# Edge columns and the isolated sources' rows moved to earlier stages of a four-layer graph kernel

## The chip, the cores and the metric

One core of a Trainium2 chip runs the whole program in one launch. The metric is device time in microseconds. The kernel before was run three times; its median is 2548.24 us.

## The reference

Four graph layers follow each other on 50,000 nodes of 128 features with 25,000 edges, sorted by destination. Each layer's result is added to its input and normalized by row (`_layernorm`).

```python
x = _layernorm(x + gat_two_layers(x, src, dst, ...))        # layer 1: two attention layers, 4 heads of 16, then 1 of 128
x = _layernorm(x + mean_of_sources(x @ W.T, src, dst) + b)   # layer 2: mean over incoming edges
m = relu(concat(x[dst], edge_attr) @ W1 + b1) @ W2 + b2      # layer 3: one message per edge
x = _layernorm(x + mean(m) @ Wm + bm + max(m) @ Wx + bx + sum(m) @ Ws + bs)
x = _layernorm(x + gat(x, src, dst, W, att, bias))           # layer 4: attention
```

A node that is no edge's destination gets only the biases in every layer. Its row can be made from its own input row alone; a source of this sort is called isolated here.

## The kernel before, in words

Edges are handled in NG = 49 groups of 512 (GT = 4 tiles of 128), not in 98 blocks of nodes. Sums over the edges of one destination are running scans along the sorted edges (`tensor_tensor_scan` on VectorE), so rows are turned into columns by transposes on PE, scanned, multiplied and turned back. The stages are separated by barriers over all five engines. Each engine's program is written out in its own order, and engines meet only in semaphores.

- **prep** (0 to 32 us) and **a** (32 to 541): indices, weights, gathers of x by source and destination.
- **b** (590 to 757, after a softmax): first attention layer in columns. `pipeline` runs `rates_vector`'s first step and `map_table` between two groups of the loop.
- **c** (757 to 1045): for each group, `look` on PE and `pick` on VectorE find the position of each source in the edge list, `hid` writes the indices, and GpSimd gathers those rows (`c_pool`, four gathers a group). Beside it VectorE and ScalarE make rows of x1 for isolated sources (`shifted`, `apply`), and VectorE runs in between what `extra` lists: the bias rows, two more edge rates and four node rates. VectorE's turn g is `hot(g+1)`, `pick(g)`, `shifted(g)`, `hid(g)`. `hot(g+1)` waits for the source digits `slb` of group g+1, which SP loads (L1457). SP's turn g is: load digits g, load rows g, store rows g-2 (L1465).
- **d** (1068 to 1285, after a softmax): second attention layer. Beside it, `local_tensor`, `local_scalar` and `local_sync` make the isolated sources' rows for layer 4: a transpose of the factors, two wide products (L1506, L1507), four scaled copies (L1524), a load and a store.
- **e** (1285 to 1564): layer 2. GpSimd gathers four times a group (L658), PE turns the rows and multiplies (L1647, L1655), VectorE scans, adds, normalizes; SP stores x2 as rows.
- **f** (1564 to 1985): layer 3, over the groups in reverse. SP loads rows of x2 and the edge features, PE turns both (`turn`), VectorE spreads each destination's last row over its edges (`spread`), PE makes hidden units and messages, VectorE scans totals and maxima (`totals`), PE combines in columns (`combine`), ScalarE and VectorE take the two results out (`columns`, L1817 and L1878), PE turns them back (`rows`, L1779), and `residual` and the normalization finish; GpSimd scatters.
- **g** and **h** (to 2540): layer 4. The change doesn't touch them.

`pipeline(engine, stages)` runs each stage in the given order for group g minus its lag, so (2, rows) works on the group two turns back. `count(engine, name, i, j, lag)` waits for the semaphore of the group `lag` back.

## Time and profile before

| | |
|---|---|
| median of 3 runs | 2548.24 us (2527.15 to 2566.37) |
| the profiled execution | 2542.37 us, span 2540.6 us |
| mean granted clock of TensorE | 0.679 |
| busy share of the span | PE 75%, VectorE (DVE) 68%, GpSimd (POOL) 54%, ScalarE (ACT) 43% |
| mean DMA rate | 157 GB/s |

Busy shares are averages over stages with different limits. A clock of 1.00 is 2.4 GHz, 0.50 is 1.2 GHz. In the timelines below each row has the start, the duration, the engine and line, what it wrote and read, and in brackets how long the engine had been idle and what ended that.

### The profile page before, as it was taken

What the parts mean: (1) busy time and instruction counts of PE and PEld (TensorE: products, weight loads), DVE (VectorE), ACT (ScalarE), POOL (GpSimd) and SP (SyncE); (2) the same over time, 40 slices, a digit from 0 to 9 for tenths busy, and PEclk for the clock granted to TensorE, in tenths of its full rate; (3) what the DMA queues carried; (4) which work ended last, traced back from release to release, by engine and by line L of the source; (5) the groups of instructions that cost most, each with busy time, mean ns of one, the idle gap of its engine ahead of it and who ended that gap; (6) DMA issues with size and microseconds to landing.
All of it is one profiled execution on the core that took longest, in us unless ns stands there. A gap on an engine that the chain in (4) does not pass through costs nothing.

```text
span 2540.6 us, 30997 instructions
## 1 busy us (share of the span) xinstructions
PE 1895.0 (75%) x7398; PEld 1202.8 (47%) x7398; DVE 1740.2 (68%) x6542; ACT 1083.8 (43%) x3008; POOL 1383.0 (54%) x1388
## 2 busy tenths in 40 slices
PE   3999999867874445399944454999998699959983
PEld 2898888855651112155534342444444122225542
DVE  6444445458769966598768885888887366678773
ACT  0222222215753343287633332666665455524332
POOL 4777777720006577200057771566666677727776
PEclk9656656655556665599756856999999555556565
DMA  4555555553334455288645554333332699933341
GB/s 154 160 155 157 155 152 160 159 188 133 125 127 125 112 156 160 72 278 262 211 131 155 154 159 120 98 112 111 109 106 82 237 363 326 313 105 100 122 135 37
DMA packets 255479, 398.63 MB, mean 157 GB/s; under 512 B 80999, under 2 KB 97536, under 8 KB 255172
## 3 DMA queue, kind: packets, MB, share of 16 engines
q1 hardware_dynamic: 204340, 307.86, 37.2%
q0 software_dynamic: 43904, 75.95, 11.0%
q10 hardware_dynamic: 7056, 12.85, 1.4%
q8 instruction: 62, 1.02, 0.2%
q14 instruction: 117, 0.96, 0.1%
HBM read 225.25 MB, written 178.97 MB: 159 GB/s over the span
## 4 chain that ended last, share of the span: by engine, by line
POOL 17%; issue 12%; PE 9%; DVE 9%; ACT 7%; DMA 3%; SPq 1%; POOLq 0%; DVEq 0%; ACTq 0%
POOL ring L658 9%; POOL big L658 4%; POOL out_dram L664 4%; ACT outr L720 3%; DVE big L1870 2%; ACT big L1809 2%; PE bank L1570 2%; DVE stats L674 2%; PE bank L1507 2%; PE bank L1506 2%; DMA ring<-x_t,idx 1%; PE bank L1211 1%; DVE z L1886 1%; DMA hT<-xsrc_e 1%; DVE mv L683 1%
## 5 line engine op out<-in xcount | busy, mean ns | idle before, releaser
L720 ACT ACTIVATE outr<-z,rn 128x128 f32<-128x128 f32 x784 | 322.7, 483 | 347.9 <-DVE rn L709 155.7
L658 POOL DMA_INDIRECT ring<-in_x_dram,idx x392 | 380.0, 969 | 147.3 <-issue 119.3
L658 POOL DMA_INDIRECT ring<-x_t,idx x280 | 269.0, 961 | 339.6 <-SPq L302 245.3
L658 POOL DMA_INDIRECT ring<-hidden_e,idx x196 | 193.3, 986 | 298.9 <-DVE idx L1361 241.6
L664 POOL DMA_INDIRECT x_t<-outr,idx x196 | 234.6, 1197 | 208.4 <-ACT outr L720 162.0
L1148 DVE TENSOR_TENSOR_SCAN G<-cont,G,bank 64x512 f32<-64x512 uint8 (+1 forms) x192 | 242.8, 1265 | 80.0 <-PE bank L1211 57.2
L664 POOL DMA_INDIRECT out_dram<-outr,idx x196 | 195.2, 996 | 102.7 <-issue 58.2
L1947 PE MATMUL bank<-DB,z 20*128 20x512 f32 x196 | 201.7, 1131 | 22.8 <-DVE xT L1337 7.0
L1020 DVE BATCH_NORM_STATS2 stats<-ring 128x6 f32<-128x128 f32 x196 | 42.8, 281 | 247.9 <-DMA ring<-in_x_dram,idx 247.9
L1301 PE MATMUL bank<-table,hT 128*128 128x391 bf16 x196 | 94.3, 481 | 153.4 <-DVE hT L1345 153.4
L674 DVE BATCH_NORM_STATS2 stats<-z 128x6 f32<-128x128 f32 x784 | 171.0, 281 | 5.1
L1211 PE MATMUL bank<-ident,msg 128*64 128x128 f32 (+1 forms) x588 | 136.3, 377 | 35.1 <-DVE msg L1133 32.2
L1570 PEld LDWEIGHTS bank<-W_s,G 65*128 65x128 f32 (+1 forms) x784 | 130.4, 252 | 65.4 <-issue 64.1
L1647 PE MATMUL bank<-ident,ring 128*128 128x128 f32 x196 | 47.8, 389 | 138.6 <-DMA ring<-x_t,idx 138.6
L1570 PE MATMUL bank<-W_s,G 65*128 65x128 f32 (+1 forms) x784 | 147.6, 348 | 0.0
L938 PEld LDWEIGHTS bank<-bT,msg 128*128 128x128 f32 x784 | 146.1, 277 | 1.0 <-ACT msg L977 0.9
L938 PE MATMUL bank<-bT,msg 128*128 128x4 f32 x784 | 143.5, 306 | 0.7 <-ACT msg L977 0.7
L977 ACT ACTIVATE msg<-bank 128x512 f32<-128x512 f32 x98 | 58.6, 598 | 188.8 <-PE bank L928 188.8
L1917 DVE CUSTOM_DVE_ANT_0 msg<-ring,attb 128x128 f32<-128x128 f32 x280 | 63.9, 288 | 101.9 <-DMA ring<-x_t,idx 59.3
L1211 PEld LDWEIGHTS bank<-ident,msg 128*64 128x64 f32 (+1 forms) x588 | 82.1, 163 | 93.1 <-issue 43.9
L658 POOL DMA_INDIRECT big<-x_t,idx x112 | 107.1, 956 | 34.2 <-issue 34.2
L716 ACT ACTIVATE sd<-mv,epsc 128x4 f32<-128x4 f32 x196 | 56.3, 287 | 157.8 <-DVE mv L683 157.8
(385 smaller groups left out, 4516.7 us busy)
## 6 DMA issues: line engine op xcount, KB each, us to landing
hT<-in_x_dram SPq DMA_DIRECT2D x194, 256.0 KB
ring<-x_e SPq DMA_DIRECT2D x147, 256.0 KB, 2.9
x_t<-outr SPq DMA_DIRECT2D x98, 256.0 KB, 2.7
x_e<-outr SPq DMA_DIRECT2D x98, 256.0 KB, 2.1
x_t<-xload SPq DMA_DIRECT2D x48, 512.0 KB, 3.1
xsrc_e<-ring SPq DMA_DIRECT2D x49, 256.0 KB, 2.1
xd_e<-ring ACTq DMA_DIRECT2D x49, 256.0 KB, 2.9
ring<-xsrc_e SPq DMA_DIRECT2D x49, 256.0 KB
```

The source lines that it names most:

```text
L658: nc.gpsimd.indirect_dma_start(to(c), None, table, bass.IndirectOffsetOnAxis(ap=idx[:, kind, (g + 1) * GT + c:(g + 1) * GT + c + 1].bitcas ...
L664: nc.gpsimd.indirect_dma_start(table, bass.IndirectOffsetOnAxis(ap=idx[:, kind, (g + 1) * GT + c:(g + 1) * GT + c + 1].bitcast(U32), axis= ...
L674: ins = v.bn_stats(stats[:, k, :], z[:, s, k, :])
L720: ins = nc.scalar.activation(to[:, k, :], frm[:, k, :], ACT.Identity, bias=sc[:, k, 1:2], scale=sc[:, k, 0:1])
L938: ins = nc.tensor.matmul(bank[4 + g % 2][:, at:at + 4], dxT[:, h, k * P:(k + 1) * P], bT[:], start=True, stop=True)
L977: nc.scalar.activation(dxT[:, q % 2, :], bank[0][:], ACT.Copy).then_inc(S("n_dxT"), 1)
L1148: return v.tensor_tensor_scan(o, m, src_ap, ini, ALU.mult, ALU.add)
L1211: ins = nc.tensor.transpose(bank[s][0:width, c * P:(c + 1) * P], msg[:, s, c, 0:width], ident[:])
L1301: nc.tensor.matmul(o, lhs, table[:, 0, :], start=True, stop=False)
L1570: ins = nc.tensor.matmul(bank[2 + s][:, c * F:(c + 1) * F], G[0:k, s, c * P:(c + 1) * P], W[:], start=not b, stop=not b or c == GT - 1)
L1917: c.do(v.tensor_tensor_reduce(msg[:, n, k, :], frm, attb[:, n, :], 1.0, 0.0, ALU.mult, ALU.add, dots[:, k, n:n + 1]))
L1947: nc.tensor.matmul(bank[2 + q % 4][:], ecT[q % 4], DB[0:GT * CN, :, :].rearrange("p t f -> p (t f)"), start=True, stop=True).then_inc(S("o ...
```

## The change

Two pieces of work move to an earlier stage, and layer 3 is rearranged around what then lies in memory.

1. The isolated sources' layer-4 rows go from d to c. They use the rows that c loads anyway (`rload`), so a load goes; a transpose, two wide products, a copy and four scaled copies go to PE and ScalarE of c, and a second store to SP of c. The edge rates and bias rows which they need go from c to b. `look` has five banks in place of six.
2. Stage e no longer stores x2 as rows. PE turns the normalized rows (`back`) and the edge features (`edges`) into columns, ScalarE copies them, and SP stores both as columns.
3. Stage f loads columns; its `turn` and the edge copy go. `combine` now has the group's columns as the stationary operand, so that it gives rows, with the two sums side by side in one bank; x2 plus bias is added by a product with the identity. The transposes back and both `columns` copies go, one copy with bias on ScalarE (`f_xb`) comes. The order of the stages on each engine is changed.

```diff
+            edge = rates_vector(v, 3, "e", ecov, est, alpha3, est, etemps)
             pipeline(v, [(-1, weighing(v, "b", feat, HF, HEADS)), (2, join), (0, scanning(v, "b", HF))],
-                     [rates_vector(v, 3, "e", ecov, est, alpha3, est, etemps)[0], map_table(v)])
+                     [edge[0], map_table(v), edge[1], rows_of_biases(v), edge[2]])
...
+        def local_tensor(pe):
+            def factors(g):
+                need(pe, "s_ecT", g)
+                nc.tensor.transpose(bank[6][0:GT * CN, 0:P], ecov[:, four(g), :].rearrange("p t k -> p (t k)"),
+                                    ident[:]).then_inc(S("s_tr"), 1)
+
+            def local(g):
+                s = g % 2
+                wait(pe, f"c_ld{g % RING}", 16 * (g // RING + 1))
+                need(pe, "s_ecT", g + 1)
+                need(pe, "s_row", g - 1)
+                nc.tensor.matmul(bank[5 + 2 * s][:], ident[:], rload[:, g % RING].rearrange("p t f -> p (t f)"), start=True, stop=False)
+                nc.tensor.matmul(bank[5 + 2 * s][:], hcT[g % 4], DB[0:GT * CN, :, :].rearrange("p t f -> p (t f)"),
+                                 start=False, stop=True).then_inc(S("s_mm"), 1)
+            return factors, local
+
+        def local_scalar(a):
...
+            def local(g):
+                need(a, "s_mm", g + 1)
+                if g >= 2:
+                    wait(a, f"s_out{g % 2}", 16 * (g // 2))
+                for k in range(GT):
+                    ins = nc.scalar.activation(sx[:, g % 2, k * F:(k + 1) * F], bank[5 + 2 * (g % 2)][:, k * F:(k + 1) * F],
+                                               ACT.Copy, scale=alpha3[:, GT * g + k:GT * g + k + 1])
+                ins.then_inc(S("s_row"), 1)
+
+        def local_store(sp, g):
+            need(sp, "s_row", g + 1)
+            sp.dma_start(edge_row(x3s_e, g), sx[:, g % 2, :]).then_inc(S(f"s_out{g % 2}"), 16)
...
             for g in range(NG):
                 look(g)
...
+                factors(g)
+                if g:
+                    local(g - 1)
+            local(NG - 1)
...
             for g in range(NG + 1):
                 if g in extra:
                     extra[g]()
                 if g < NG:
+                    factors(g)
+                if g:
+                    local(g - 1)
+                if g < NG:
                     apply(g)
...
             for g in range(NG + 2):
                 if g < NG:
                     load(g)
...
                 if g >= 2:
                     store(g - 2)
+                    local_store(sp, g - 2)
...
-            pipeline(pe, [(0, turn), (1, project)])
+            def edges(i, j):
...
+                for c in range(GT):
+                    ins = nc.tensor.transpose(bank[6 + s][0:EF, c * P:(c + 1) * P], e_ea[:, s, c, :], ident[:])
...
+            def back(i, j):
...
+                for c in range(GT):
+                    ins = nc.tensor.transpose(bank[4 + s][:, c * P:(c + 1) * P], outr[:, j, c, :], ident[:])
+                ins.then_inc(S("e_xtr"), 1)
+            pipeline(pe, [(0, turn), (1, project), (1, edges), (3, back)])
...
+            return (0, load), (4, store)
...
+                nc.scalar.activation(e_eaT[:, s, :], bank[6 + s][0:EF, :], ACT.Copy).then_inc(S("e_eaT"), 1)
...
+                nc.scalar.activation(e_xT[:, s, :], bank[4 + s][:], ACT.Copy).then_inc(S("e_xT"), 1)
+            pipeline(a, [(2, step), (2, edges), (4, back)])
...
+                sp.dma_start(f_x[:, j], x2T_e[g]).then_inc(S(f"f_xs{j}"), 16)
+                count(sp, "f_m1", i, j, RING)
+                sp.dma_start(f_ea[:, j], eaT_e[g]).then_inc(S(f"f_xs{j}"), 16)
...
-                nc.tensor.matmul(bank[4][:], Mm_s[:], G[:, s, :], start=True, stop=True)
-                nc.tensor.matmul(bank[5][:], Ms_s[:], G[:, s, :], start=True, stop=False)
-                nc.tensor.matmul(bank[5][:], Mx_s[:], MX[:, s, :], start=False, stop=True).then_inc(S("f_mm2"), 1)
...
+                for c in range(GT):
+                    o = f_rows(s, c)
+                    e = slice(c * P, (c + 1) * P)
+                    nc.tensor.matmul(o[:, 0:2 * F], G[:, s, e], MmMs[:], start=True, stop=False)
+                    nc.tensor.matmul(o[:, F:2 * F], MX[:, s, e], Mx_s[:], start=False, stop=False)
+                    ins = nc.tensor.matmul(o[:, F:2 * F], aT[:, s, e], ident[:], start=False, stop=True)
+                ins.then_inc(S("f_mm2"), 1)
+            pipeline(pe, [(-1, hidden), (0, message), (1, combine)])
+
+        def f_rows(s, c):
+            return bank[4 + s + 2 * (c // 2)][:, (c % 2) * 2 * F:(c % 2 + 1) * 2 * F]
...
-                nc.scalar.activation(aT[:, s, :], bank[4][:], ACT.Copy).then_inc(S("f_aT"), 1)
+                nc.scalar.activation(aT[:, s, :], X2T[:, j, :], ACT.Identity, bias=m3c[:]).then_inc(S("f_xb"), 1)
...
-            pipeline(a, [(0, relu), (-1, edges), (3, apply), (0, message), (2, means), (1, columns), (2, root)])
+            pipeline(a, [(-1, relu), (0, message), (3, apply), (0, columns), (2, means), (2, root)])
...
-                v.scalar_tensor_tensor(bT2[:, s, :], bank[5][:], m3c[:], X2T[:, j, :], ALU.add, ALU.add) \
-                    .then_inc(S("f_bT"), 1)
...
-            pipeline(v, [(3, scale), (-1, spread), (0, penalty), (0, totals), (2, residual), (2, norm_stats(v, "f")),
-                         (2, norm_var(v, "f")), (1, columns)])
+                for n in range(2):
+                    rows = bank[4 + s + 2 * n][:].rearrange("p (t n f) -> p t n f", t=2, n=2)[:, :, 1, :]
+                    ins = v.tensor_tensor(z[:, s, 2 * n:2 * n + 2], rows, zA[:, s, 2 * n:2 * n + 2], ALU.add)
+                ins.then_inc(S("f_z"), 1)
+            pipeline(v, [(3, scale), (-2, spread), (0, penalty), (0, totals), (2, residual), (2, norm_stats(v, "f")),
+                         (2, norm_var(v, "f"))])
```

## Rows read from the trace of the kernel before

**Rows 1.** Windows: us; busy PE, PEld, DVE, ACT, POOL (count); clock, DMA, GB/s.

```profile
757.00:1045.00 288.00, 121.53 (x392) 46.78 (x392) 212.40 (x658) 106.09 (x301) 193.28 (x196) 0.62 0.49 135
...
1068.00:1284.50 216.50, 206.52 (x833) 110.90 (x833) 176.27 (x637) 148.39 (x491) 0.00 (x0) 0.85 0.75 237
1284.50:1564.00 279.50, 120.70 (x588) 107.20 (x588) 218.41 (x839) 90.11 (x245) 188.70 (x196) 0.65 0.51 151
1564.00:1985.00 421.00, 370.66 (x1372) 186.93 (x1372) 330.24 (x784) 250.40 (x637) 234.58 (x196) 0.96 0.33 98
...
1100.00:1130.00 30.00, 29.80 (x138) 16.13 (x138) 28.81 (x105) 24.13 (x82) 0.00 (x0) 1.00 0.89 283
```

**Rows 2.** Instructions of one line, f: duration ns, first and last start us.

```profile
L1148 DVE TENSOR_TENSOR_SCAN G<-cont,G,hT x48: 1282/1284/1337, 1582.1 to 1952.6; 128x512 f32<-128x512 uint8 x48
```

**Rows 3.** Timeline of stage f, one group and the next scan.

```profile
1743.33 0.38 DVE L683 BATCH_NORM_AGGREGATE mv<-stats 128x2 f32<-128x6 f32 x4
...
1743.62 0.72 DVE L1878 SCALAR_TENSOR_TENSOR big<-bank,m3c,big 128x512 f32<-128x512 f32 x1
1743.74 0.30 ACT L716 ACTIVATE sd<-mv,epsc 128x4 f32<-128x4 f32 x1 [2.06 <-DVE mv L683]
...
1744.99 1.64 ACT L720 ACTIVATE outr<-z,rn 128x128 f32<-128x128 f32 x4
...
1745.35 1.02 PE L1759 MATMUL bank<-hT,M_s 128*128 128x512 f32 x2
...
1746.53 0.67 ACT L1800 ACTIVATE hT<-bank,m2c 128x512 f32<-128x512 f32 x1
...
1747.10 1.12 ACT L1809 ACTIVATE big<-bank,invR 128x128 f32<-128x128 f32 x4
1747.24 1.28 DVE L1148 TENSOR_TENSOR_SCAN G<-cont,G,hT 128x512 f32<-128x512 uint8 x1 [1.07 <-ACT hT L1800]
```

**Rows 4.** Timeline of stage c: GpSimd around the node layers, then one ring.

```profile
810.87 0.94 POOL L658 DMA_INDIRECT ring<-hidden_e,idx  x1 [0.57 <-DVE idx L1361]
...
870.70 2.66 POOL L658 DMA_INDIRECT ring<-hidden_e,idx  x1 [2.85 <-DVE idx L1361]
...
908.25 0.95 POOL L658 DMA_INDIRECT ring<-hidden_e,idx  x1 [0.30 <-issue]
...
916.47 0.42 ACT L1427 ACTIVATE big<-ring 128x256 f32<-128x256 f32 x1 [4.85 <-DMA ring<-hidden_e,idx]
...
918.55 0.32 SPq L1465 DMA_DIRECT2D x_t<-outr  x1
...
919.50 0.42 ACT L1427 ACTIVATE big<-ring 128x256 f32<-128x256 f32 x1 [0.97 <-DMA ring<-hidden_e,idx]
...
923.19 0.35 DVE L1345 TENSOR_SCALAR hT<-hT,pcol 128x512 bf16<-128x512 bf16 x1 [3.54 <-DMA hT<-srclo_d]
...
926.49 0.16 DVE L1361 SCALAR_TENSOR_TENSOR idx<-hidt,dhi 128x4 int32<-128x4 f32 x1
```

**Rows 5.** Timeline of stage d: its last scan.

```profile
1270.53 1.27 DVE L1148 TENSOR_TENSOR_SCAN G<-cont,G,bank 64x512 f32<-64x512 uint8 x1 [2.69 <-PE bank L1211]
```

**Rows 6.** Groups by line: busy us, mean ns, idle before.

```profile
L1240 ACT ACTIVATE hT<-G,b1c 64x512 f32<-64x512 f32 x49 | 34.6, 706 | 0.0
...
L1886 DVE TENSOR_TENSOR z<-bank,big 128x512 f32<-128x512 f32 x49 | 32.7, 667 | 5.6 <-ACT big L1809 5.6
...
L1129 DVE TENSOR_TENSOR msg<-big,alpha 128x256 f32<-128x256 f32 x49 | 19.2, 394 | 0.1
...
L1379 DVE SCALAR_TENSOR_TENSOR DB<-biasc,ident,DB 32x128 f32<-32x128 f32 x12 | 4.1, 340 | 0.4
```

**Rows 7.** Timeline of stage b: PE behind a rate layer.

```profile
667.83 1.97 PE L1221 MATMUL bank<-W2x,hT 64*128 64x66 f32 x8 [8.09 <-DVE hT L1199]
```

**Rows 8.** Timeline of stage e: residual and mask.

```profile
1412.34 1.13 DVE L1671 SCALAR_TENSOR_TENSOR z<-bank,invR,ring 128x128 f32<-128x128 f32 x4 [0.36 <-PE bank L1655]
...
1414.11 0.16 DVE L709 TENSOR_TENSOR rn<-rn,lastR 128x8 f32<-128x8 f32 x1
```

More of the change, by code:

```diff
@@ L1191, in map_table, with rows_of_biases, step @@
             return step
+        def rows_of_biases(v):
+            ch = Chain(v)
+            def step():
+                for t in range(GT):
+                    for k, n in ((0, 1), (1, 2), (2, 3), (3, None), (4, 0)):
+                        row = ones[0:32, :] if n is None else biasc[0:32, n, :]
+                        at = ident[0:32, CN * t + k:CN * t + k + 1]
+                        if k == 0:
+                            ch.link(v.tensor_scalar(DB[:, t, :], row, at, None, ALU.mult))
+                        else:
+                            ch.link(v.scalar_tensor_tensor(DB[:, t, :], row, at, DB[:, t, :], ALU.mult, ALU.add))
+            return step
         def b_vector(v):
@@ L1369, in shifted @@
                     .then_inc(S("c_z"), 1)
-            def rows_of_biases():
-                for t in range(GT):
-                    for k, n in ((0, 1), (1, 2), (2, 3), (3, None), (4, 0)):
-                        row = ones[0:32, :] if n is None else biasc[0:32, n, :]
-                        at = ident[0:32, CN * t + k:CN * t + k + 1]
-                        if k == 0:
-                            ch.link(v.tensor_scalar(DB[:, t, :], row, at, None, ALU.mult))
-                        else:
-                            ch.link(v.scalar_tensor_tensor(DB[:, t, :], row, at, DB[:, t, :], ALU.mult, ALU.add))
-            edge = rates_vector(v, 3, "e", ecov, est, alpha3, est, etemps)
             node = rates_vector(v, 4, "n", cross, stat, alpha4, None, ntemps)
@@ L1387, in scaled @@
                 v.sem_inc(S("n_scaled"), 1)
-            extra = {3: rows_of_biases, 5: edge[1], 7: edge[2], 9: node[0], 11: node[1], 13: node[2], 15: node[3],
-                     16: scaled}
+            extra = {9: node[0], 11: node[1], 13: node[2], 15: node[3], 16: scaled}
             hot(0)
@@ L1573, in attend_tensor @@
             wait(pe, tag + "_ones", 1)
[L1574 to L1578 removed]
+            pipeline(pe, [(0, turning(pe, tag, width)), (1, project)])
         def attend_scalar(a, tag, stored):
@@ L1586, in step @@
                 norm_apply(z[:, s], outr[:, j], rn[:, s]).then_inc(S(tag + "_row"), 1)
-            if tag == "d":
-                factors, local = local_scalar(a)
-                pipeline(a, [(-1, factors), (1, local), (0, step)])
-            else:
-                groups(a, step)
+            groups(a, step)
         def attend_pool(pool, tag, table, kind, rev):
@@ L1624, in linear_sync @@
             if more is None:
-                pipeline(sp, [(-2, load), (3, store)] + list(also))
+                pipeline(sp, [(-2, load)] + ([(3, store)] if to is not None else []) + list(also))
             else:
@@ L1689, in step, with edges, back @@
                 count(a, "e_st", i, j)
-                slot_done(a, "e_out", i, j, 16, 1)
+                need(a, "e_xtr", RING * i + j + 1 - RING)
                 norm_apply(z[:, s], outr[:, j], rn[:, s]).then_inc(S("e_row"), 1)
-            groups(a, step)
-        eaR = ring[:, 0:2, 1, :, 0:EF]
+            def edges(i, j):
+                g = RING * i + j
+                s = g % 2
+                need(a, "e_eatr", g + 1)
+                if g >= 2:
+                    wait(a, f"e_out{(g - 2) % RING}", 16 * ((g - 2) // RING + 1))
+                nc.scalar.activation(e_eaT[:, s, :], bank[6 + s][0:EF, :], ACT.Copy).then_inc(S("e_eaT"), 1)
+            def back(i, j):
+                g = RING * i + j
+                s = g % 2
+                need(a, "e_xtr", g + 1)
+                if g >= 2:
+                    wait(a, f"e_xo{(g - 2) % RING}", 16 * ((g - 2) // RING + 1))
+                nc.scalar.activation(e_xT[:, s, :], bank[4 + s][:], ACT.Copy).then_inc(S("e_xT"), 1)
+            pipeline(a, [(2, step), (2, edges), (4, back)])
+        f_x = ring[:, :, 0].rearrange("p s t f -> p s (t f)")
+        f_ea = ring[0:EF, :, 1].rearrange("p s t f -> p s (t f)")
         def f_sync(sp):
@@ L1727, in store @@
                 sp.dma_start(edge_row(x3_e, g), outf[:, j, :]).then_inc(S(f"f_out{j}"), 16)
-            pipeline(sp, [(-1, load), (3, store)])
+            pipeline(sp, [(-3, load), (3, store)])
             for j in range(RING):
@@ L1732, in f_tensor @@
         def f_tensor(pe):
[L1733 to L1745 removed]
             def hidden(i, j):
[L1748 removed]
                 count(pe, "f_spread", i, j)
[L1750 removed]
+                wait(pe, f"f_xs{j}", 32 * (i + 1))
                 count(pe, "f_relu", i, j, 1)
                 nc.tensor.matmul(bank[2][:], M1a[:], X2T[:, j, :], start=True, stop=False)
[L1753 removed]
+                nc.tensor.matmul(bank[2][:], M1b[:], f_ea[:, j], start=False, stop=True).then_inc(S("f_m1"), 1)
             def message(i, j):
@@ L2014, in _ @@
             barrier(sp)
-            linear_sync(sp, "d", xd_e, x1_e, False, "_z", also=local_sync(sp))
-            for s in range(2):
-                sp.wait_ge(S(f"s_out{s}"), 16 * len(range(s, NG, 2)))
+            linear_sync(sp, "d", xd_e, x1_e, False, "_z")
             barrier(sp)
-            linear_sync(sp, "e", x1_e, x2_e, False, "_z")
+            linear_sync(sp, "e", x1_e, None, False, "_z", also=e_turn_sync(sp))
+            for j in range(RING):
+                wait(sp, f"e_out{j}", 16 * (BODIES + (j == 0)))
+                wait(sp, f"e_xo{j}", 16 * (BODIES + (j == 0)))
             barrier(sp)
```

237 lines of the change are left out of this document (65 added, 172 removed), and 2 rows, old and new, of the table SHARED.

## Prediction

> **What bounds the kernel now.** I read the windows by stage first, then in each stage the change touches the timeline of a few groups, asking which wait ends last. The span is 2540.6 us; the profiled execution as a whole took 2542.4 us, 5.9 under the median of 2548.2 shown. The change touches stages b to f [rows 1]. In **f** VectorE starts its totals scan every 7.88 us ((1952.6 - 1582.1) / 47) [rows 2]. VectorE is not full: it waits 1.07 us for ScalarE's message in each group [rows 3]. The reader is to see a ring: VectorE adds m3c (L1878), PE transposes the rows and only then makes the message (L1759), ScalarE adds its bias (L1800), VectorE scans, and so back to L1878 [rows 3]. In **c** each gather takes 0.95 us and the next follows after 0.30, so four make 5.0 us a group. GpSimd is just about the bound, but a second ring has little slack. For one group it reads: gather issued from 908.25, rows copied at 916.47, mean layer's apply, SP's store at 918.55, then SP's load of the source digits, for which VectorE waits until 923.19, index ready at 926.65 [rows 4]. That is 18.4 us for four groups' time, 20.0: the copy of group g-4 releases the index of group g, because apply(g-2) stands behind copy(g-4) on ScalarE and the digits of g+1 stand behind store(g-2) on SP. In **d** the windows show PE busy 207 of 216 us, and VectorE 28.8 of 30 us where the clock is 1.00 [rows 1]. In **e** GpSimd issues the gathers at 1.25 us, 5.0 us a group, and VectorE is busy 218 of 280 us [rows 1, 4].
>
> **Stage f.** VectorE loses `columns` (0.72 us, 0.64 from its start to the next) and gets the residual in two halves. A 128x512 one takes 0.67, a 128x256 operation 0.39, so two cost 0.79, 0.12 more [rows 6]. But `columns` was what covered the square root between the variances and the next reciprocal: from the start of the variances (1743.33) to the end of the root (1744.04) is 0.71, where `columns` started after 0.29 [rows 3]. So 7.89 - 1.07 - 0.64 + 0.12 + 0.45 = 6.75, with what the halves add in starts 6.8. ScalarE's order changes too: apply and a copy from SBUF now stand between message and means. From the variances' start: root at 0.41, relu 0.2 later, message and apply 0.57 after each (1747.10 - 1746.53), so apply 1.75, columns 3.29 (1.54 for apply, from 1744.99 to 1746.53), then 0.63 (the nearest row, a 64x512 from SBUF, takes 0.71 with its tail) and four means of 1.12 together: ready at 5.05, just where VectorE wants them (5.02: 0.74 to the reciprocal, 0.31 for the scale, 1.6 for spread and penalty, 2.37 for the two totals scans) [rows 3, 6]. PE: column passes fall from 8192 to 7168 a group, so its busy 7.56 (370.7 / 49) becomes at most 6.6, and the clock, 0.96, stays as the load does [rows 1]. I take 6.83: (7.88 - 6.83) x 47 = 49 saved; bounds 6.65 and 7.15, which are 58 and 34. The transposes that vanish from the start are made good by one more stage of lead. The loads sit behind the same 3.1 MB of `cont`.
>
> **Stage d.** It loses a transpose, two wide products and five ScalarE instructions a group. From its first scan, 1.4 us into the stage, to its last at 1270.53 there are 48 steps of 4.19 us [rows 1, 5]. At full clock 105 VectorE instructions in 30 us are 8.1 groups of 13, 3.71 each [rows 1]. VectorE's work does not depend on the clock, and what PE keeps (four transposes, four fp32 products in two passes each, twelve passes of 128 columns) fits 3.7 us even at half the clock: a pass of 512 takes 0.43 at the upper level (1.02 for two with their tail [rows 3]), so one of 128 at the lower 0.21, and twelve 2.6. 48 x 0.48 = 23 saved, and about 6 in the drain, where two wide products at half clock went before the last rows: 29; bounds 22 and 33.
>
> **Stage b.** It gains two rate layers and the twenty instructions for the bias rows. The rate layer that is there held up the product by 8.09 us [rows 7]; the two others are shorter (one and no later term): 7 and 6. Twenty instructions of 0.34 plus a wait each are 7.4, less 0.7 of VectorE's slack in a group [rows 6]. The index table, moved to the middle, no longer waits for its prefix products at the end, about 3.5. Sum 7 + 6 + 6.7 - 3.5 = 16 lost; bounds 12 and 20.
>
> **Stage c.** What it loses on VectorE is worth about 4 us, since GpSimd ran on. What it gains is: on PE a transpose and two wide fp32 products; on ScalarE a copy of the factors and four scaled copies (together some 1.3 us); on SP one more 256 KB store a group. None is long. The costly part is **where they stand**. `local_store(g-2)` waits for ScalarE's `local(g-2)`, which is in ScalarE's turn g-1, behind copy(g-3). Behind that wait on SP are the digits of g+1, and behind those VectorE's index of g. So the ring that spanned four groups spans three. Its length: from gather to copy 8.2; copy, factors and local 1.7, where apply had 2.1; stores 0.4 and digits 4.3; hot, pick, shift and index 3.5: 18.1 us [rows 4], or 6.05 a group in place of 5.0. When the gather lands quickly (group 25 began at 913.25 and was copied at 919.50, 6.3 against 8.2) it is 16.2, or 5.4. I take 6.05, because the burst of SP's transfers now follows every copy and meets the gather in flight. Eight groups (9 to 17) take 59.8 us, 810.87 to 870.70 [rows 4], bound by VectorE's node layers, and don't change. Three start without the ring. The 48 steps from the first group's gather to the last's are 270 of the stage's 288 us (9 go by before the first index, 9 from the last gather on) [rows 1]; they become 59.8 + 15 + 37 x 6.05 = 299: 29 lost. Bounds: 5.4 gives 4, and 7.0 gives 64.
>
> The clock is the other term in c. Now it is 0.62 with PE busy 122 of 288 us; in d, nearly full, 0.85; in f 0.96 [rows 1]. 
> **Stage e.** PE gets eight transposes, ScalarE two copies (0.58 and 0.60), SP a load and a second store. Two things could end the cover. On ScalarE the next root now stands behind apply and both copies: 1.54 + 0.5 + 0.5 + 0.33 = 2.9 us from the start of apply to the reciprocal, 0.1 to the residual, 1.77 from there to the mask (1412.34 to 1414.11) and 0.2 to the next apply: 4.9 in all against 5.0, so I cost them at nothing [rows 3, 8]. PE's work at half clock is twenty passes of 128, 4.3 us of 5.0. The drain gets a transpose, a copy and a store: 3 lost; bounds 0 and 18. The transfers add 256 KB a group to a DMA share of 0.51 [rows 1]. The edge rows are 256 bytes each; the Trainium skill ("DMA: Bandwidth & Descriptors", Specifications) gives 512 B as the least transfer for line rate. By that rule this load costs about twice its bytes, still within the free share, so it speaks for the fourth rival alone; no row of e shows it, since such loads run only in f.
>
> **Sum.** 16 + 29 - 29 + 3 - 49 = -30. Against the profiled execution 2512; against the median of the runs 2518. All bounds at once give -75 and +46; they won't all fall together.
>
> **Rivals.** (1) The ring in c doesn't bind and GpSimd sets 5.0 a group. For it: SP's waits cost others little now, and in every second group the gather lands fast. Against it: the count of turns above. 59.8 + 40 x 5.0 is 10 less than before: -69, so 2479. (2) The other side: the burst (256 KB store, digits, 256 KB load) lengthens its own ring. The digits and the gather then land some 2 us later each, 21.9 in place of 18.1, 7.3 a group: c loses 75 and the sum is +16, 2564. It decides from 6.86 a group on, where c has eaten the rest. Against it: the DMA share in c is 0.49. (3) In f the means come late (ScalarE's longer order, a dearer SBUF copy): 7.3 a group, 22 us less gain, 2540. (4) The edges aren't hidden beside e's gathers: ScalarE's chain of 4.9 or the small rows make 5.5 a group, 24 us more, 2542; then the change doesn't do what it says.
>
> **Chances.** Forecast 0.45 with its own range of 2495 to 2540; rivals 0.20, 0.12, 0.13 and 0.10. A measurement of this kernel can tell about 2% (51 us) from no change. Faster by more is most of rival 1 and the forecast's low edge, 0.26; slower by more needs rival 2 and a second mishap, 0.06. The range goes from rival 1 to past rival 2, with the 20 us by which the runs differ.
>
> **What the changed profile would show.** f: totals scans 6.8 us apart, no wait of VectorE for ScalarE's message, 0.4 us of wait before the reciprocal. c: outside the node layers 6.05 between groups, GpSimd waiting for the index in each, VectorE waiting for the digits, SP waiting for the sx copies. d: scans 3.7 apart at whatever clock. e: still 1.25 between gathers. I am wrong if c stays at 5.0 (rival 1), if PE's clock in f falls below 0.9, or if e's gathers show gaps.

## The result and the profile after

The changed kernel is slower, by 1.2 to 2.2%. In four runs of each, side by side, its median is 2570.4 us (2569.7 to 2574.1) and that of the kernel before 2537.7 (2520.9 to 2566.4); the ratio is 1.017, 95% interval 1.012 to 1.022. Here and below, medians are of all executions, while ratios and their intervals leave out those more than 1.5% above the fastest of the same kernel. The two profiled executions differ by 28 us: 2570.8 against 2542.4 us, spans of 2569.0 and 2540.6.

The table gives each stage in these two profiles. The marks are the first scan of stage b, VectorE's first hot mask (the start of c's lookups), its last one, the first scan of e, the last one, the first running maximum of f, and the first dot product of g.

| stretch | before | after | change | predicted |
|---|---|---|---|---|
| b, first scan to first hot mask | 168.1 | 185.3 | +17 | +16 |
| c, first to last hot mask | 264.6 | 306.9 | +42 | +29 |
| rest of c and d, to e's first scan | 268.7 | 231.9 | -37 | -29 |
| e, first to last scan | 244.1 | 297.0 | +53 | 0 |
| e's drain and f's start | 41.3 | 48.2 | +7 | +3 |
| f, from its first maximum to g | 417.7 | 368.0 | -50 | -49 |

The rest (a before, g and h behind) differs by 4 us in the other direction, and with it the rows add up to the 28 us of the spans. Four terms are about where they were put. Two are not: c, and above all e.

The windows of the changed kernel, to be read against [rows 1]; the rows are stages b, c, d, e and f.

```profile
core 0: us, PE busy (x) PEld busy (x) DVE busy (x) ACT busy (x) POOL busy (x), PEclk, DMA share, GB/s
587.00:772.00 185.00, 143.91 (x589) 114.06 (x587) 131.87 (x205) 116.17 (x254) 0.00 (x0) 0.51 0.28 108
772.00:1092.00 320.00, 242.17 (x637) 82.27 (x637) 200.23 (x625) 164.56 (x541) 188.83 (x196) 0.73 0.55 160
1092.00:1303.00 211.00, 139.61 (x602) 117.98 (x602) 184.78 (x667) 99.33 (x253) 0.83 (x2) 0.50 0.38 124
1303.00:1627.50 324.50, 184.04 (x980) 166.11 (x980) 218.41 (x838) 142.05 (x343) 187.25 (x196) 0.69 0.56 159
1627.50:2024.00 396.50, 344.56 (x1481) 211.95 (x1481) 309.76 (x784) 232.43 (x607) 243.84 (x204) 0.91 0.39 120
```

In e (fourth row) no engine is near full: VectorE does the same 218 us of work as before in 45 us more, and GpSimd's 187 us of gathers are spread over 324. So something else ends last there. The waits of the changed kernel from e's first scan to its last say what (us in total, times, longest):

```profile
PE bank L1615 <- ACT hT L1689: 105.9, 41, 4.6
ACT outr L720 <- DVE rn L709: 99.9, 46, 3.3
DVE rn L692 <- ACT sd L716: 76.9, 41, 3.2
ACT hT L1689 <- DMA eaT_e<-hT: 56.3, 43, 2.6
...
POOL ring L658 <- PE bank L1597: 43.7, 23, 3.0
```

The fourth row is the root and the others are what it drags along. ScalarE's copy of the edge columns (L1689) waits in 43 of 49 groups for the store of the columns two groups back to land. (The landing of a transfer is meant from its issue to the release of the engine that waits for it.) TensorE's next edge transposes wait for that copy, VectorE's reciprocal for the root behind it, and GpSimd's gathers for TensorE's turn (L1597), which is the gap between gathers that the prediction named as the sign of its being wrong.

The timeline of the changed kernel, one turn in e:

```profile
1445.73 0.59 ACT L1689 ACTIVATE hT<-bank 64x512 f32<-64x512 f32 x1 [1.89 <-DMA eaT_e<-hT]
1446.22 0.58 ACT L1697 ACTIVATE hT<-bank 128x512 f32<-128x512 f32 x1
1446.83 0.32 SPq L1648 DMA_DIRECT2D x2T_e<-hT  x1
1447.19 0.43 SPq L1557 DMA_DIRECT2D ring<-x_t  x1
1447.67 0.50 SPq L1637 DMA_DIRECT2D hT<-in_edge_attr_dram  x1
1448.21 0.49 SPq L1646 DMA_DIRECT2D eaT_e<-hT  x1
1449.48 0.94 POOL L658 DMA_INDIRECT ring<-x_t,idx  x1 [2.64 <-PE bank L1597]
1453.33 0.59 ACT L1689 ACTIVATE hT<-bank 64x512 f32<-64x512 f32 x1 [2.59 <-DMA eaT_e<-hT]
```

It is a ring of **one** turn. The copy (1445.73), the back copy behind it on ScalarE (1446.22), SyncE's store of the node columns, which waited for the back copy (1446.83), two loads behind that store, and only then the store of the edge columns (1448.21), whose landing releases ScalarE's next copy (1453.33). From copy to issue is 2.5 us in all but the last few turns; from issue to the next copy it is 5.1 us here, 4.4 and 3.0 in the turns on either side. The 49 copies run from 1325.55 to 1621.57, 6.2 us apart, so the landing takes 3.7 on average. The chain of waits that ended last, over the same stretch, says the same in one line, for the changed kernel and then for the kernel before:

```profile
by line: DMA eaT_e<-hT 51.1%; issue 11.4%; POOL ring L658 8.1%; ACT hT L1697 7.9%; SPq L1637 6.5%; SPq L1557 5.7%; SPq L1648 4.2%; DMA ring<-x_t,idx 1.4%; ACT hT L1689 0.7%; PE bank L1605 0.6%; ACTq L291 0.5%; DVE z L1661 0.4%; PE bank L159
```
```profile
by line: POOL ring L658 74.2%; issue 23.5%; DMA ring<-x_t,idx 1.2%; POOLq L302 0.5%; PE bank L1647 0.5%; PE bank L1655 0.3%
```

Before, GpSimd's gathers and the gaps between them are 98% of the chain. After, the landing and the five instructions of the ring are three quarters. Over the whole stage the landings that a copy waits for take 2.3 to 5.1 us, 3.8 in the mean. The Trainium skill ("DMA: Bandwidth & Descriptors", Anatomy of one DMA) gives, for transfers issued by GpSimd, about 2.0 us of fixed cost, most of it the write's receipt, and the bytes at 436 GB/s: 2.3 us for these 128 KB, an estimate by that page. The trace is above it in every turn shown, and comes down to it only once, at the end of the stage. This store is in flight beside gathers and behind 640 KB that SyncE issued just ahead. The 256 KB store of the node columns, which has no other issue close ahead of it, lands in 2.1 us (median) in the same stage; that what stands ahead makes the difference is likely, and not shown.

In c the predicted ring is there. In the changed kernel, SyncE's store of the isolated rows (L1345) stands ahead of the digits (L1475), and VectorE's mask (L1386) waits for them; compare [rows 4]:

```profile
956.62 1.09 ACT L1338 ACTIVATE xT<-bank,dlo 128x128 f32<-128x128 f32 x4
957.73 0.32 SPq L1345 DMA_DIRECT2D x_t<-xT  x1
958.10 0.43 SPq L1475 DMA_DIRECT2D hT<-srclo_d  x1
958.26 0.16 DVE L1402 SCALAR_TENSOR_TENSOR idx<-hidt,dhi 128x4 int32<-128x4 f32 x1
...
961.98 0.35 DVE L1386 TENSOR_SCALAR hT<-hT,pcol 128x512 bf16<-128x512 bf16 x1 [3.55 <-DMA hT<-srclo_d]
```

### The profile page after: what moved, and what is told of

Read it like the earlier page. It is cut to its first block, busy times and chain, and to the rows that moved or that the text cites. A ratio compares the mean times of both kernels' runs of the same rounds, so it can differ in the third digit from the quotient of the medians.

```text
span 2569.0 us, 32122 instructions
## 1 busy us (share of the span) xinstructions
PE 1978.2 (77%) x7888; PEld 1327.5 (52%) x7888; DVE 1715.9 (67%) x6541; ACT 1125.9 (44%) x3061; POOL 1379.5 (54%) x1388
## 4 chain that ended last, share of the span: by engine, by line
DVE 12%; POOL 11%; issue 10%; ACT 9%; DMA 8%; PE 3%; SPq 2%; POOLq 0%; ACTq 0%; DVEq 0%
DMA eaT_e<-hT 6%; POOL out_dram L664 4%; POOL big L658 4%; DVE stats L674 3%; ACT outr L720 3%; POOL ring L658 3%; DVE G L1148 2%; ACT big L1777 2%; DVE z L1847 1%; DVE mv L683 1%; DVE z L1512 1%; DMA ring<-x_t,idx 1%; ACT big L1785 1%; ACT hT L1697 1%; ACT hT L1763 1%
## 5 line engine op out<-in xcount | busy, mean ns | idle before, releaser
L1226 PE MATMUL bank<-ident,msg 128*64 128x128 f32 (+1 forms) x588 | 154.1, 417 | 68.6 <-DVE msg L1133 65.6
L1528 PEld LDWEIGHTS bank<-W_s,G 65*128 65x128 f32 (+1 forms) x784 | 166.2, 312 | 65.8 <-issue 63.4
L1528 PE MATMUL bank<-W_s,G 65*128 65x128 f32 (+1 forms) x784 | 183.7, 411 | 0.4 <-DVE G L1148 0.4
L1355 PE MATMUL bank<-table,hT 128*128 128x391 bf16 x196 | 87.4, 446 | 72.1 <-DVE hT L1386 71.3
L1226 PEld LDWEIGHTS bank<-ident,msg 128*64 128x64 f32 (+1 forms) x588 | 89.6, 177 | 102.9 <-DVE msg L1133 81.0
L1615 PE MATMUL bank<-ident,hT 128*64 128x128 f32 x196 | 42.2, 357 | 110.0 <-ACT hT L1689 110.0
L1749 PE MATMUL bank<-MmMs,G 128*128 128x256 f32 x392 | 121.4, 392 | 6.7 <-DVE z L1847 3.3
```

Of the source, the lines that this page charges most:

```text
L1226: ins = nc.tensor.transpose(bank[s][0:width, c * P:(c + 1) * P], msg[:, s, c, 0:width], ident[:])
L1355: nc.tensor.matmul(o, lhs, table[:, 0, :], start=True, stop=False)
L1528: ins = nc.tensor.matmul(bank[2 + s][:, c * F:(c + 1) * F], G[0:k, s, c * P:(c + 1) * P], W[:], start=not b, stop=not b or c == GT - 1)
L1749: nc.tensor.matmul(o[:, 0:2 * F], G[:, s, e], MmMs[:], start=True, stop=False)
```

## Experiments

All are compared with the kernel before, run beside them. The first nine kernels met a condition that the first pair had not: every kernel, the one before too, took 2.91 to 2.97 ms, with idle time on VectorE, ScalarE and TensorE at once that nothing in the trace releases (see the last section). In the eight after that the kernel before was back at 2536 and 2543 us. Both are told, since the first kernels misled me about c. "Distance" is the mean time between VectorE's scans (e) or hot masks (c).

### First set: one limit at a time

**The store of the edge columns one turn earlier.** SyncE issues it as soon as the copy is done, ahead of that turn's wait for the back copy:

```
+            def store_ea(i, j):
...
+                need(sp, "e_eaT", g + 1)
+                sp.dma_start(eaT_e[g], e_eaT[:, g % 2, :]).then_inc(S(f"e_out{j}"), 16)
...
-            return (0, load), (4, store)
+            return (0, load), (3, store_ea), (4, store)
```

> In the changed kernel ScalarE's copy of a group's edge columns waits 44 times for the landing of the store of the columns two groups back (56.5 us in all). SyncE issues that store behind the store of the node columns of the turn before, which itself waits for ScalarE, so the wait closes a ring of one turn. Here the store of the edge columns is issued one turn earlier and nothing else changes. Theory (the ring sets stage e): the forward scans come 5.0 to 5.3 us apart instead of 6.19, ScalarE's waits for that landing fall below 10 us, and the time falls by 42 to 57 us, to 2513 to 2528 us. Rival (the waits fill time that transfers at a share of .56 and a TensorE clock of .69 cost anyway): the scans stay above 5.9 us and the time at 2555 us or more.

Measured: distance 6.38 us in e, no wait for that landing among the large ones, 2923.4 us, ratio 0.991 (0.986 to 0.995).

**The same store first in its turn.** It stays at lag 4 but goes ahead of the two loads.

> A smaller dose of the same. The store of the edge columns stays at its turn but goes ahead of that turn's two loads (0.43 + 0.50 us of issue). The ring of one turn stays and loses about 1.0 us. Theory: scans 5.1 to 5.4 us apart, time lower by 38 to 52 us than the changed kernel, and some wait for the landing stays (10 to 40 us in all). Rival (transfers and clock): scans above 5.9 us, time at 2555 us or more. A second rival (SyncE's order matters by what is queued ahead in the queues, not by the time of issue) would give the same as the run with the earlier turn, with no wait left.

Measured: 6.50 us, 2940.9 us, ratio 0.993 (0.988 to 0.998). The distances of both runs are on the side of the rival (above 5.9 us). The times say nothing by themselves, since both theory and rival had been worked out for the conditions of the first pair.

**c: the store of the isolated rows one turn later.**

```
-            for g in range(NG + 2):
+            for g in range(NG + 3):
...
-                if g >= 2:
+                if 2 <= g < NG + 2:
                     store(g - 2)
-                    local_store(sp, g - 2)
+                if g >= 3:
+                    local_store(sp, g - 3)
```

> Only stage c changes: the store of the isolated sources' rows goes three turns behind the loads instead of two, so that it no longer holds the next digits load until ScalarE's rows of the turn before are done. Theory (a ring of three groups, 20 us long, sets c): the ring has four groups again, hot masks come 5.2 to 5.9 us apart instead of 6.65, first to last gather 274 to 295 us instead of 314, time lower by 19 to 40 us than the changed kernel (2530 to 2551 us). Rival (TensorE at 1.2 GHz, with 8.6 us of matmuls a group at that clock, sets c): first to last gather stays at 300 us or more and the time at 2556 us or more.

Measured: 6.55 us in c, 2949.0 us, ratio 0.998 (0.995 to 1.001). The expectation gives 6.65 us for the changed kernel; its masks of the first profile are 6.39 us apart, so this is no gain at all.

**Both edits.**

> Both edits together. Theory: they are in different stages and add up, 61 to 97 us less than the changed kernel, 2473 to 2509 us, that is 1 to 3% faster than the kernel before. Rival (one or both of the rings were not what set their stages): 2520 us or more.

Measured: 6.60 us in c, 6.51 in e, 2941.4 us, ratio 0.993 (0.989 to 0.997). Taken alone, this set spoke for the rivals. What was missing were the unaltered kernels under the same conditions.

### Second set: the unaltered kernels, and what is left in e

> The changed kernel once more, unaltered, so that the next three have it beside them on the same chip and day. Scans of stage e 6.2 to 6.7 us apart, hot masks of stage c 6.3 to 6.7, ratio to the kernel before 1.00 to 1.02 whatever the theory.

Measured: 6.64 us in e, 6.39 in c, 2933.7 us, ratio **0.994** (0.990 to 0.998). Under these conditions the change doesn't lose, against the expectation's 1.00 to 1.02.

> With the edge columns' store one turn earlier the scans of stage e were still 6.38 us apart, against 6.63 in a run with that stage unaltered, and the waits had moved: TensorE's edge transposes now wait 20 times for the landing of the attributes' load, which SyncE issues one turn ahead behind the node columns' store. Here that load goes two groups ahead as well, into four buffers instead of two (the store of the edge columns stays one turn earlier). Theory (ScalarE's back copy, SyncE, a landing, TensorE or ScalarE again: rings of one or two turns through SyncE's order set the stage): scans 5.0 to 5.5 us apart, time 33 to 55 us under the changed kernel on this chip. Rival (the gathers of this stage with a transfer share of .56, and TensorE's clock, set it): still 6.1 us or more, time less than 20 us under it.

```
-                need(sp, "e_eatr", g - 1)
+                need(sp, "e_eatr", g - 3)
...
-            return (0, load), (4, store)
+            return (-2, load), (3, store_ea), (4, store)
```

Measured: 6.33 us, 2923.8 us, ratio 0.992 (0.988 to 0.995): 10 us under the changed kernel, which is the rival's figure.

> Leaves out of stage e all work on edge attributes (their load, the four transposes, ScalarE's copy and the store); stage f then loads raw attributes in place of their columns, so its messages are of other numbers at the same sizes. What is left in stage e of the move are the node columns. Theory (the edge columns' ring is what stage e lost): scans 5.0 to 5.4 us apart, time 38 to 60 us under the changed kernel. Rival (the node columns' part, four transposes, a copy of 0.58 us and a 256 KB store, costs as much or more): 5.8 us or more, time less than 25 us under it.

Measured: 6.13 us, 2915.2 us, ratio 0.987 (0.981 to 0.993): 19 us under it, the rival's figure too.

> Stage c with the rows' store at three turns and without the matmul of the identity with the loaded rows (1.9 us a group at 1.2 GHz, 1.0 at 2.4), so that the isolated sources' rows lack the sources' own part. With the store at three turns alone the hot masks came 6.55 us apart, no closer than before. Theory (the ring of three groups and TensorE at 1.2 GHz lie level at 6.5 to 6.7 us a group, so that one edit alone shows nothing): 5.2 to 5.9 us apart, time 25 to 55 us under the changed kernel. Rival (landings of the digits and of the gathers set the stage, whatever TensorE does): 6.3 us or more, time less than 12 us under it.

Measured: 6.33 us in c, 2934.3 us, ratio 0.994 (0.990 to 0.998): no change, again the rival's figure.

> The kernel before once more, unaltered, for its profile. In the runs so far both kernels take 2.93 to 2.97 ms where the first pair took 2.54 and 2.57, and the changed kernel's profile of those runs has idle time ahead of an engine that ends with nothing that the trace shows, up to 22 us long, which its first profile has not. Theory (instructions arrive late there, in both kernels): this profile has such gaps too, stage a some 200 us longer than in the first profile of this kernel, and the scans of stage e 5.6 to 6.4 us apart in place of 4.98, since a stage that was set by its engines' own work loses more by it than one that waits for landings anyway. Rival (the gaps belong to the changed kernel's code): no such gaps, scans 5.0 us apart.

Measured: 2963.4 us; the same kernel beside it took 2912.8, so one execution here can be 50 us off another. e 6.01 us (5.09 in the first profile, where the expectation, dividing 47 steps by 48, has 4.98), c 6.08, stage a 211 us longer than in the first profile, b within 1 us and f's maxima 7.81 us apart as they were. Waits of ScalarE over the whole run, kernel before, in the first profile and then in this one:

```profile
ACT msg L977 <- PE bank L928: 188.8, 98, 9.9
```
```profile
ACT msg L977 <- remote: 175.4, 21, 14.4
ACT z L1960 <- issue: 132.5, 77, 13.6
ACT outr L720 <- issue: 129.8, 62, 4.0
```

So all of e's changes must be read between 6.01 (before) and 6.64 (after): 6.64 unaltered, 6.50 store first, 6.38 store a turn earlier, 6.33 load earlier too, 6.13 without edges, 6.01 before. Each is one profile. The store a turn earlier came out again in the kernel with both edits, at 6.51, so differences of 0.13 us say nothing, while three profiles with an unaltered e agree within 0.03 (6.63 to 6.66). The edges are 0.51 of the 0.63 us, and the ring 0.13 to 0.26 of them. It binds, but other idle time covers most of it.

### Third set: doubling the suspected cost

```
+                sp.dma_start(eaT2_e[g], e_eaT[:, s, :]).then_inc(S(f"e_out{j}"), 16)
                 sp.dma_start(eaT_e[g], e_eaT[:, s, :]).then_inc(S(f"e_out{j}"), 16)
```

> The changed kernel with the store of the edge columns issued twice, the second to a tensor that nobody reads, and ScalarE's copy waiting for both. It lengthens the ring of one turn by one issue of 0.5 us and by what the landing of 128 KB more takes. Theory (the ring binds in most groups): the scans of stage e come 0.5 to 1.2 us further apart than in the unaltered changed kernel of these runs (6.64), so 7.1 to 7.8 us, time 20 to 55 us longer than it. Rival (transfer load alone): under 6.9 us, the same growth as in the next run.

> The same doubling in the kernel in which that store goes one turn earlier (6.38 us between scans). Theory: the landing has a turn to spare there, so the doubling costs only what the extra transfer takes from others, 0 to 0.3 us a group. Rival (transfer load sets the stage): the scans move apart by as much as in the run before.

These ran without that idle time. Doubled in place: 2594.6 us, ratio 1.026 (1.019 to 1.034). Doubled with the store a turn earlier: **2516.1 us, ratio 0.994** (0.990 to 0.998), 54 us under the changed kernel although it stores 128 KB more in every group. (The changed kernel's 2570.4 us are of the first pair, whose kernel before took 2537.7; here it took 2536.1.) The scans of e in the kernel before, in the changed kernel, then in these two (first and last start after the commas):

```profile
L1148 DVE TENSOR_TENSOR_SCAN G<-cont,G,bank x48: 1246/1280/1282, 1298.5 to 1537.7; 128x512 f32<-128x512 uint8 x48
```
```profile
L1148 DVE TENSOR_TENSOR_SCAN G<-cont,G,bank x48: 1246/1248/1282, 1315.4 to 1608.2; 128x512 f32<-128x512 uint8 x48
```
```profile
L1149 DVE TENSOR_TENSOR_SCAN G<-cont,G,bank x48: 1245/1248/1281, 1318.1 to 1630.2; 128x512 f32<-128x512 uint8 x48
```
```profile
L1149 DVE TENSOR_TENSOR_SCAN G<-cont,G,bank x48: 1244/1249/1281, 1319.0 to 1559.8; 128x512 f32<-128x512 uint8 x48
```

Counted from the first scan of all, which these lines leave out, the distances are 5.09, 6.19, 6.59 and 5.10 us. In the ring the second store costs 0.40 us a group, less than the 0.5 to 1.2 expected: about its issue of 0.5 us, and no time of its own to land. Outside the ring it costs nothing. The rival's "under 6.9 us" is met, its "same growth" in the second kernel is not, and that is what tells the two apart: transfer load as the cause is out. ScalarE's wait for the landing, in the kernel doubled in place, against 56.3 us above:

```profile
ACT hT L1691 <- DMA eaT_e<-hT: 77.1, 43, 2.9
```

> Part 1 of the change alone (the isolated sources' rows beside stage c) on the kernel before. By the stages of the two unaltered kernels in runs of this kind: stage b 16 us longer, stage c's hot masks 15 us longer in all, from the last of them to the first scan of stage e 52 us shorter, so 18 to 24 us less than the kernel before. If the parts act on each other (for instance through TensorE's clock), the stages come out otherwise. In the first pair the same stages add up to 23 us more.

Measured: 2562.4 us, ratio 1.014 (1.006 to 1.021), so slower, not faster: it ran under the first pair's conditions, in which the expectation names 23 us more, and 26 over the 2536.1 of the kernel before came out. b is 185.3 us, c 308.1, and e 5.12 us a group, as before: part 1's costs stay in b and c.

> Part 2 alone (columns made in stage e, read in f) on the kernel before, with the edge columns' store one turn earlier and the attributes' load two groups ahead into four buffers. Theory: stage e 15 to 25 us longer than in the kernel before (scans 6.2 to 6.3 us apart against 5.9), stage f 50 us shorter, so 25 to 35 us less than the kernel before, a ratio of 0.988 to 0.992. Rival (the gains in e of this mending are noise of single profiles): stage e 37 us longer as in the changed kernel and a ratio of 0.995 or more.

Measured: 2502.2 us (2471.7 to 2523.9), ratio 0.983 (0.971 to 0.994). e is 5.05 us a group, no longer than before and not the 6.2 to 6.3 expected, for the same reason.

### Fourth set: what sets c, and the version to keep

> Both edits again (the edge columns' store of e one turn earlier, the isolated rows' store of c one turn later), because the last four runs had no gaps of late instructions and the first try of it had. Stage e 5.1 us a group in either case, so 2516 us if c stays at 6.4 us a group. Theory (the ring of three groups sets c): hot masks 5.3 to 5.9 us apart, 2465 to 2493 us. Rival (TensorE, with 6.7 us from the first look of a group to its last matmul at 1.2 GHz): 6.1 us or more, 2502 us or more.

> Stage e mended as above; stage c keeps its order, and the matmul of the identity with the loaded rows is left out (the isolated sources' rows lack the sources' own part): 1.9 us less of TensorE a group at 1.2 GHz. Theory (the ring sets c, and that matmul lies in it only where ScalarE waits for TensorE, 19 times in the first profile): hot masks 6.0 to 6.4 us apart. Rival (TensorE sets it): 5.2 to 5.8 us.

> All three: the store of the isolated rows one turn later, and the identity's matmul left out. Theory (either limit alone holds c at some 6 us, both gone give the kernel before's distance): 5.2 to 5.6 us a group, 2460 to 2480 us. Rival (a third limit, such as the landings of digits and gathers beside 256 KB more of stores a group): 5.9 us or more, 2495 us or more.

| kernel (all with e mended) | c, distance | time | ratio (95%) |
|---|---|---|---|
| c's store a turn later | 5.45 | 2476.3 | 0.977 (0.971 to 0.982) |
| c without the identity's matmul (the isolated rows lack the source's own part) | 6.43 | 2518.1 | 0.992 (0.989 to 0.995) |
| both | 5.47 | 2475.5 | 0.976 (0.970 to 0.981) |

The order alone gives all of it, 42 us against the second row and 40 against the doubled kernel above, whose e is mended too; the identity's matmul gives nothing. The third row's figures are those of its theory, but the reason given there, two limits that each hold c, is refuted by the first row. The store still stands right ahead of the digits' load in the first row, so it is the wait in front of it that costs, not its bytes. The masks and what they waited for, in the changed kernel and with c's store a turn later:

```profile
L1386 DVE TENSOR_SCALAR hT<-hT,pcol x49: 348/353/567, 772.4 to 1079.3; 128x512 bf16<-128x512 bf16 x49
its engine sat idle before it (us, times) until:
  DMA hT<-srclo_d: 117.8, 40
```
```profile
L1386 DVE TENSOR_SCALAR hT<-hT,pcol x49: 348/353/579, 775.9 to 1037.6; 128x512 bf16<-128x512 bf16 x49
its engine sat idle before it (us, times) until:
  DMA hT<-srclo_d: 72.6, 40
```

GpSimd waited 34 times for an index in that stretch of the changed kernel, and 6 times here. In e the gathers lead the chain of the mended kernel again:

```profile
by line: POOL ring L658 61.4%; issue 20.9%; DMA ring<-x_t,idx 3.9%; DVE z L1664 2.3%; DMA hT<-in_edge_attr_dram 2.0%; ACT outr L720 1.5%; PE bank L1606 1.4%; DVE z L1672 1.3%; PE bank L1598 1.1%; ACT hT L1692 0.9%; ACT hT L1700 0.8%; PE ban
```

> The version that should beat both kernels: part 2 alone on the kernel before, with the edge columns' store one turn earlier and nothing else. Theory: stage e 6 to 12 us longer than in the kernel before (the drain), stage f 50 us shorter: 38 to 44 us less than the kernel before, a ratio of 0.983 to 0.986. Rival (part 1 gave stage d 35 us that part 2 alone lacks, and d varies by 30 us between runs of the kernel before): within 1% of the changed kernel with the same mending, 2516 us.

Measured: 2490.8 us, ratio 0.981 (0.975 to 0.987). The expectation's 38 to 44 us came out as 47 to 52 (its kernel before was at 2542.6). The lowest median has the whole change with both stores moved by a turn: 2476.3 us, 2.3% under the kernel before and 94 us under the change as it was made. That it beats part 2 alone is not shown: the intervals overlap, and part 2's six executions, which keep the old stage d, go from 2471 to 2507 us where its four lie within 7.

## Why the prediction failed

**Stage e is the step that failed.** The prediction "cost them at nothing", with 3 us for the drain. Its sum of 4.9 against 5.0 us was a sum of ScalarE's **work** (apply, two copies, root) with VectorE's and had no wait in it. The two copies write into two buffers each, and each waits for the store of two groups back. Lag 2 for the copy and lag 4 for the store leave no turn between them: the copy of group g needs the store of g-2, which SyncE issues behind its wait for the back copy of the turn just before. This is the very count of turns that the prediction made for `local_store` in c, and did not make for the second store in e. It came to 53 us over 48 steps and 6 in the drain (13.6 to 19.3 us from the last scan to f's first load). Shown: the chain, the wait that grows when the store is doubled, and the 1.1 us a group that go when only the turn changes (three kernels whose stage e differs in nothing else have 5.09 or 5.10). The fourth rival had the place and the sign at half the size (24 us), with the wrong causes, ScalarE's full turn and small rows. ScalarE is busy 142 of 324 us, and with the store a turn earlier the stage runs at 5.1 us with the same rows to load. So that rival's mechanism is refuted too.

**Stage c: the mechanism was right, its size short.** Predicted +29 us, measured +42 by the masks. The steady part was right: from index 16 (890.71) to index 48 (1085.79) there are 6.10 us a group, predicted 6.05, and before 5.03 (870.26 to 1031.31). That is 34 of the 42 us. The rest is where the prediction held things as they were: the eight groups with the node layers, 59.8 us before, took 65.4 (825.31 to 890.71), and the first eight 48.2 instead of 45.5. The 4 us that the prediction names for work that VectorE loses stand in no term of its sum. From the first group's gather to the last's, which is what its sum counts, it had 270 us before and 299 after; the trace has 270 and 310. The first rival (the ring doesn't bind) and the second (7.3 us a group) are out, and the store a turn later, which gives 5.45 us back, shows the ring. TensorE's lower clock, held in the bounds, did not set the distance: without the identity's matmul it is the same.

**Stage d: right, a little short.** Scans come 3.56 us apart, predicted 3.71, before 4.19, at a granted clock of 0.50: "at whatever clock" held. The gain is 37 us, predicted 29, against this one profile of the kernel before: the same stretch with the same code took 259 to 299 us in four profiles (see the last section), so a part of the match is luck.

**Stage b: right**, +17 for +16.

**Stage f: right.** The maxima come 6.78 us apart, predicted 6.83, and from the first of them to g 50 us are gone, predicted 49. The granted clock over the stage's window is 0.91, and 0.99 from 1656 to 1982, between the first maximum and the last. The fork over ScalarE's longer order (third rival) did not open. Around one turn, VectorE has the predicted short wait before the reciprocal and none before the totals scan:

```profile
1700.42 0.18 DVE L692 RECIPROCAL rn<-sd 128x4 f32<-128x4 f32 x1 [0.36 <-ACT sd L716]
...
1702.33 1.28 DVE L1148 TENSOR_TENSOR_SCAN G<-cont,G,hT 128x512 f32<-128x512 uint8 x1
```

So the forecast's -30 became +28: of the 58 us between them 57 are e with its drain and 13 are c, while d gives 8 and the stretch ahead of b 5 back. The result, 2570, lies where the prediction lets its range end, "past rival 2" (2564); that width came from c's bounds, not from what made the kernel slow, so as far as it reaches the result it is luck.

## What to carry to other kernels

When a step gains a buffer that a transfer empties, write down for each wait the turn in which its releaser is issued, and what stands ahead of that issue in the queue's order. A store that lags its producer by as many turns as there are buffers closes a ring as long as its landing, and no sum of busy times shows it. Adding a wait for a late engine to a queue that also issues early loads costs all who need those loads. Moving one line of the queue's order was worth 54 us here, and another 40, with no work taken away. And before reading an experiment, run and profile both unaltered kernels beside it.

## What the runs showed that I had not expected

- **Three engines can stand idle together with nothing that releases them, and it hides other limits.** In the profiles of nine kernels on three chips, VectorE, ScalarE and TensorE were all idle 26 to 37 times for 2.5 to 16 us at a time, in the stages with gathers (a, c, e, g) and in h, and not in b, in f, or in the changed kernel's d. The trace names no releaser. The other ten profiles have no such stop. One such stop in stage c, of the kernel with the later store and without the identity's matmul, all three resuming within 0.8 us:

```profile
1197.88 0.62 DVE L1391 SCALAR_TENSOR_TENSOR msg<-iota,shi,bank 128x391 bf16<-128x391 f16 x1 [4.26 <-issue]
...
1198.57 0.51 PE L1354 MATMUL bank<-table,hT 128*128 128x391 bf16 x1 [3.35 <-issue]
...
1198.67 0.27 ACT L1330 ACTIVATE hT<-bank 20x128 f32<-20x128 f32 x1 [5.01 <-remote]
```

  That the queues that bring instructions are the cause is argued from this, not shown. The kernel before took 420 us more with it and the changed one 363, so the ratio turned from 1.017 to 0.994. By one profile of each, c grew by 27 us before and by nothing after, and e by 44 and 22, which fits that stages that wait for landings anyway lose less; another 16 us of the difference are the kernel before's stage d, told next. An edit worth 54 us in one condition showed 10 in the other, and one worth 40 showed none; why is not shown.
- **Stage d of the kernel before has no fixed time.** With the isolated rows in it, its scans came 4.04 us apart at a granted clock of 0.91, 4.19 at 0.85, 4.47 at 0.80 and 4.82 at 0.74 (in this order: part 2 alone, the kernel before twice, and part 2 alone with the deeper load), with TensorE busy for 95 to 98% of the stage. Without them they come 3.55 or 3.56 apart, and the clock is 0.50. The changed kernel's four runs lie within 4.4 us and the other's within 45, which fits; that it is all of the spread is not shown.
- **A second store on the heels of the first cost 0.40 us a group**, less than the 0.5 us of its own issue, so its landing added nothing that shows.
